# Full-height products, earlier maxima and a load behind a row of maxima in an attention stack

## The chip, the core and the metric

The kernel runs on one core of one Trainium2 chip. The metric is the device time of one execution in microseconds (us). TensorE's array has 128 rows; a product whose contraction has 64 terms uses 64 of them. TensorE's clock is granted at one of two levels, 1.2 or 2.4 GHz; the profile gives it as a share of the higher.

## The reference, cut to what matters

Four layers over 1024 tokens of width 256, each `x = x + attention(xn) + ffn(xn)` with `xn = layernorm(x)`. The change touches layer 0, and the order of work in layer 2. Layer 0's attention has 16 heads with low-rank queries and keys and a rotary part:

```python
ql, kvl = xn @ Wqd, xn @ Wkvd              # latents of 64 features each
q_nope, q_rope = ql @ Wqu, rope(ql @ Wqr)  # 16 and 64 features a head
k_nope, v = kvl @ Wku, kvl @ Wvu
k_rope = rope(xn @ Wkr)                    # one for all heads
# causal softmax of [q_nope q_rope].[k_nope k_rope], times v, times Wo
```

Beside it runs layer 0's second branch, again causal attention with 16 query heads against one key and value head that a router has selected for each token. Layer 2 has plain 16-head causal attention. Layer 1's feed-forward has a Hadamard transform, which the kernel folds into the weights `w_dn`.

## The kernel before, in words

All engines run their own instruction streams in order and meet at semaphores. Attention goes in groups of four heads: groups 0 to 7 in layer 0, even ones with the rotary part ("MLA"), odd ones of the shared key; groups 8 to 11 in layer 2. A group goes over eight key tiles, written (group, tile). For each tile TensorE writes scores to PSUM `psA` (MLA: lines 1678 and 1679), ScalarE writes their exponentials to `Pr` (lines 907 and 912), GpSimd masks the diagonal block (776), and TensorE multiplies the tile before by the values into `psO` (1716). Tiles 0 to 3 have four score units of up to 1024 queries, tiles 4 to 7 two of two heads each.

The softmax subtracts row maxima that come from a coarse pass of its own, done beside the tiles of the group before: 38 units a group, each a bf16 product (1661) into `psD` with a mask product (1663) on the diagonal, which VectorE reduces to `mx` (1199). `max_window` says beside which tiles the units go and `beside` spreads them by the queries left in each tile. At tile `MAX_END` = 5 the maxima are negated (1204), transposed (1669), copied to `mrow` (1217) and sent by a DMA in ScalarE's queue into the query operand, where they are a further row (926 and 929, `maxima_row`). The next group's first score waits for that DMA (`mrow_in`).

MLA operands come back from DRAM: SyncE's queue holds, for each even group i, the stores of two rotated tiles (`store_rotated`), a wait for the scores of (i, 3), `load_high(i + 2, 0)` (the high parts of the first 512 queries and keys, three DMAs: `Qr<-d_qr`, `Qr<-d_qn`, `Kr<-d_kn`), a wait for the group's last score, and then `load_high(i + 2, 1)` and all the rest. TensorE's `arrived(i + 2)` waits for the first three before the first maxima unit of group i + 2, which stands right behind the first score of (i + 1, 0).

Before group 0 the order is the list `PRE0`: the latents, the key rotation, two of four nope products, the rotated queries (four tiles, four `rope_unit`s each, f32 products in pairs, line 1595), and then the 38 maxima units of group 0 with other products among them: the values `v0` after unit 28, nope 1 after 31, nope 3 after 34. The four other tiles of rotated queries are made beside (2, 0), (2, 2), (4, 0) and (4, 2). Latents lie in one tile `lat`, queries in rows 0 to 63 and keys in rows 64 to 127. At the start of group 7 TensorE waits for GpSimd's butterflies (787) and makes four units of the Hadamard product (1759), which VectorE scales (1245).

Of the kernel before, what the change touches and what calls it, by code (L numbers as in the profile page):

```python
# [51 lines left out]
MAX_UNITS = list(max_units())  # L52
MAX_END = 5

# [21 lines left out]
def beside_products(i, kt):  # L76

    if (i, kt) in KV_AT:
        return [("kv", j) for j in KV_AT[i, kt]]
    if (i, kt) in ROPE_AT:  # L80
        return [("rope", ROPE_AT[i, kt], k) for k in range(4)]
    return []


def max_window(i, first):

    if i == 1:
        return [(0, kt) for kt in range(KEY_KT, MAX_END)]
    tail = [(i - 2, kt) for kt in range(MAX_END, NT) if i - 2 >= first and not is_mla(i)]
    return tail + [(i - 1, kt) for kt in range(MAX_END)]  # L90

# [23 lines left out]
def build(nc, ins, out):  # L115
    with ExitStack() as ctx:
# [119 lines left out]
        w_u, w_vu = part(D), part(D)  # L236
        w_o0, w_g0, w_qkv0 = part(DC, D), part(DC, H), part(DC, 3 * D)
        w_qkv0_at = 2 * DC * P + 2 * H * RD + 2 * D + DC * D + DC * H
        part = carve(WA)
# [138 lines left out]
        def d_attention(groups):  # L378

            names = [(f"max{groups[0]}", NMAX), (f"mrow{groups[0]}", 1)]  # L380
            for i in groups:
                nxt = i + 1 if i + 1 in groups else None
                if i == 2 * NG - 1:
                    names.append(("wdn", FC // 2))
                for kt in range(NT):
                    if nxt is not None and kt == MAX_END:
# [61 lines left out]
        dve_step, pool_step = sem("dve_step"), sem("pool_step")  # L448
        v_cleared, rotated = sem("v_cleared"), sem("rotated")
        ln_var, ln_std, xn_ready = sem("ln_var"), sem("ln_std"), sem("xn_ready")  # L450
# [30 lines left out]
        def _(sp):  # L481
# [13 lines left out]
            load(w_u[0:LAT, :], ins["Wqu"], w0_in)  # L495
            load(w_u[LAT:P, :], ins["Wku"], w0_in)
            load(w_vu[LAT:P, :], ins["Wvu"], w0_in)
# [91 lines left out]
            for i in GROUPS[0]:  # L589
# [4 lines left out]
                if is_mla(i) and i < 2 * NG - 2:  # L594

                    if i > 0:
                        store_rotated(i + 2)
                        store_rotated(i + 3)
                    sp.wait_ge(rope_stored, 16 * 2 * (i + 2))
                    sp.wait_ge(a_filled, scored(i, NT // 2 - 1))  # L600
                    load_high(i + 2, 0)
                    sp.wait_ge(a_filled, A[f"att{i}"])
                    load_high(i + 2, 1)
                    load_rest(i + 2, 0)
                    load_rest(i + 2, 1)
# [254 lines left out]
        def _(act):  # L860
# [31 lines left out]
            def attention(groups):  # L892
                for i in groups:
                    for kt in range(NT):
# [21 lines left out]
                        if (i, kt - 1) in ROPE_AT:  # L916
                            rope_cut(ROPE_AT[i, kt - 1])
                        if kt == MAX_END and i + 1 in groups:
                            maxima_row(i + 1)
# [199 lines left out]
        def _(dve):  # L1119
# [117 lines left out]

            def down_weights():

                dve.wait_ge(w1_in, 16 * N_W1)  # L1240
                for u in range(FC // 2):
                    src = take().rearrange("p (j d) -> p j d", j=2)
                    for k in range(2):
                        m = 2 * u + k
                        op = dve.scalar_tensor_tensor(w_dn[:, m, :], src[:, k, :], su[:, DC + m:DC + m + 1], ws_dp,
                                                      ALU.mult, ALU.mult)
                    op.then_inc(d_drained, 1)

# [11 lines left out]
            def attention(groups):  # L1260
# [6 lines left out]
                for i in groups:  # L1267
                    nxt = i + 1 if i + 1 in groups else None
                    if i == 2 * NG - 1:
                        down_weights()  # L1270
                    for kt in range(NT):
                        if nxt is not None and kt == MAX_END:
                            maxima_row(nxt)
                        for j in KV_AT.get((i, kt), ()):
                            if j == 0:
# [31 lines left out]
            def biased_times(dst, other, half, bias):  # L1307
# [3 lines left out]


            link(dve.memset(mx[:], LOWEST))
            stats()
            norm()
            dve.wait_ge(wq_high_ready, 1)
            dve.tensor_tensor(wq_low[0:LAT, :], WA[0:LAT, 2 * DC * P:2 * DC * P + 2 * T], wq_high[0:LAT, :],
                              ALU.subtract).then_inc(q_parts_ready, 1)
# [252 lines left out]
        def _(pe):  # L1571
# [173 lines left out]
            def attention(groups):  # L1745
# [7 lines left out]
                for i in groups:  # L1753
                    nxt = i + 1 if i + 1 in groups else None
                    if i == 2 * NG - 1:

                        pe.wait_ge(butterflies, 1)
                        for u in range(FC // 2):
                            pe.matmul(d_unit(), had[:], fT8[:, 2 * u:2 * u + 2, :].rearrange("p c d -> p (c d)"),
                                      start=True, stop=True).then_inc(d_filled, 1)  # L1760
                    if is_mla(i):
# [7 lines left out]
                    for kt in range(NT):  # L1769
# [12 lines left out]
                        def some_maxima(p):  # L1782
                            for unit in ahead[p * len(ahead) // points:(p + 1) * len(ahead) // points]:
# [3 lines left out]
                                if unit[0] == "kv":  # L1787
                                    selected_unit(unit[1])
                                    continue
                                if unit == MAX_UNITS[0]:  # L1790
                                    arrived(g)
# [3 lines left out]
                        for k, hs in enumerate(heads):  # L1795
                            one(hs)
                            if nxt is not None and kt == MAX_END:
                                if k == 1:
# [38 lines left out]
            def rope_unit(p, k):  # L1837
# [3 lines left out]
                product(d_unit(), [(wq_high[:, tile_cols(m)], lat_parts[:, c]),  # L1841
                                   (wq_low[0:LAT, tile_cols(m)], lat_parts[0:LAT, c])]).then_inc(d_filled, 1)

# [16 lines left out]
            pe.wait_ge(a_drained, A["xnT0"])  # L1860
            ql = lambda k, c: lat[0:LAT, c]
            kvl = lambda k, c: lat[LAT:P, c]
            for item in PRE0:
# [7 lines left out]
                elif item[0] == "nope":  # L1871
                    u = item[1]
                    pe.wait_ge(a_drained, A["lat"])
                    if u < 2:
                        features(lambda k: w_u[0:LAT, tile_cols(u)], ql, [0])
                    else:
                        features(lambda k: w_u[LAT:P, tile_cols(u - 2)], kvl, [0])
                elif item[0] == "v0":
                    value_units(kvl, lambda k: w_vu[LAT:P, :], [0])
                elif item[0] == "rope":  # L1880
# [238 lines left out]
```

## Time and profile before

| | us |
|---|---|
| median of 3 runs | 1012.65 (1007.17 to 1013.95) |
| the profiled execution, its own time | 1012.09 |
| its span | 1010.0 |
| mean granted clock of TensorE | 0.897 |

The span is from the first to the last instruction of the one profiled execution; 2.1 us lie around it. Everything read from the trace belongs to that execution. Landmarks on its time axis: PRE0 to 95, groups 0 to 7 from 95 to 478, groups 8 to 11 from 691 to 820.

### The profile page before, as it was taken

The page shows a single profiled execution, that of the slowest core. Times are in us where ns is not written, and L with a number is a line of the kernel's source. Part 1 is how long each engine was busy: PE and PEld are TensorE (multiplying, and loading weights), DVE is VectorE, ACT ScalarE, POOL GpSimd, SP SyncE. Part 2 cuts the span into 40 slices and gives each one's busy share as a digit, 9 for nine tenths or more (in the row PEclk, how much of TensorE's full clock was granted, in tenths as well). Part 3 has the DMA queues.
Part 4 walks back from the last instruction along what each step waited for, and adds up shares of the span by engine and source line. Part 5 has one row for each costly group of instructions (what it writes and reads, how often), then busy time and mean ns, then how long its engine had stood idle before and what let it go on. Part 6 is the DMA issues. An engine that isn't in the chain of part 4 may idle for free.

```text
span 1010.0 us, 11938 instructions
## 1 busy us (share of the span) xinstructions
PE 889.0 (88%) x4799; PEld 511.0 (51%) x4799; DVE 559.2 (55%) x988; ACT 387.0 (38%) x476; POOL 224.8 (22%) x207
## 2 busy tenths in 40 slices
PE   4998979999999899979589998977999889978997
PEld 2453534344334434424337877623333258778776
DVE  4583566774566367621443355496777426945452
ACT  2503424444443435445441431214556763500340
POOL 2381001323012301342210100400111236610010
PEclk9675999999698969989788998967999989979899
DMA  6675414532921390020400002477100051000001
GB/s 171 132 159 200 63 31 72 119 73 75 156 32 43 94 210 17 1 71 1 146 0 1 1 1 86 107 144 113 17 2 1 1 217 44 1 1 1 1 1 42
DMA packets 35647, 66.81 MB, mean 66 GB/s; under 512 B 5908, under 2 KB 14652, under 8 KB 35524
## 3 DMA queue, kind: packets, MB, share of 16 engines
q1 hardware_dynamic: 35016, 65.92, 28.3%
q8 instruction: 38, 0.62, 0.3%
q10 hardware_dynamic: 576, 0.13, 0.1%
q14 instruction: 17, 0.14, 0.0%
HBM read 45.93 MB, written 16.29 MB: 62 GB/s over the span
## 4 chain that ended last, share of the span: by engine, by line
PE 67%; DVE 19%; ACT 5%; DMA 4%; POOL 2%; issue 2%; SPq 1%; ACTq 0%; DVEq 0%; POOLq 0%
PE psD L1595 12%; PE psA L1595 11%; PE psO L1716 10%; DVE mx L1199 9%; PE psD L1661 9%; PE psO L1595 8%; PE psA L1679 7%; PE psA L1678 3%; DVE hid_low L1509 2%; PE psD L1663 2%; ACT Pr L907 1%; PE psA L1627 1%; DMA Kr<-d_kn 1%; ACT Pr L912 1%; PE psD L1727 1%
## 5 line engine op out<-in xcount | busy, mean ns | idle before, releaser
L1199 DVE TENSOR_REDUCE mx<-psD 128x1 f32<-128x512 f32 (+3 forms) x416 | 259.2, 658 | 127.8 <-PE psD L1663 91.1
L907 ACT ACTIVATE Pr<-psA 128x1024 f32<-128x1024 f32 (+3 forms) x192 | 161.8, 866 | 200.4 <-PE psA L1679 191.0
L776 POOL TENSOR_SCALAR_AFFINE_SELECT Pr<-Pr 128x512 f32<-128x512 f32 x96 | 60.9, 635 | 441.2 <-ACT Pr L907 355.1
L912 ACT ACTIVATE Pr<-psA 128x1024 f32<-128x1024 f32 (+3 forms) x96 | 63.5, 702 | 65.4 <-PE psA L1679 65.0
L1716 PE MATMUL psO<-Pr,Vh 128*32 128x512 f32 (+3 forms) x768 | 82.5, 510 | 3.7 <-POOL Pr L776 3.0
L1678 PE MATMUL psA<-Qr,Kr 128*128 128x512 f32 (+3 forms) x192 | 78.8, 424 | 2.8 <-DMA Qr<-mrow 2.8
L1663 PE MATMUL psD<-maskq,identb 128*128 128x128 bf16 x348 | 73.0, 234 | 0.0
L1679 PE MATMUL psA<-Qr,Kr 113*128 113x512 f32 (+3 forms) x192 | 67.1, 357 | 0.0
L1661 PE MATMUL psD<-Kr,Qr 80*128 80x512 bf16 (+3 forms) x166 | 60.2, 395 | 5.3 <-DVE mx L1199 3.0
L1661 PE MATMUL psD<-Kg,Qs 96*128 96x512 bf16 (+3 forms) x192 | 56.9, 337 | 8.6 <-DVE mx L1199 6.6
L1661 PE MATMUL psD<-Ks,Qs 96*128 96x512 bf16 (+3 forms) x166 | 53.5, 351 | 4.6 <-DVE mx L1199 3.9
L1679 PE MATMUL psA<-Qs,Kg 97*128 97x512 bf16 (+3 forms) x192 | 50.1, 357 | 7.2 <-DMA Qs<-mrowb 4.8
L1679 PE MATMUL psA<-Qs,Ks 97*128 97x512 bf16 (+3 forms) x192 | 45.8, 332 | 5.3 <-ACT Pr L907 3.3
L1678 PEld LDWEIGHTS psA<-Qr,Kr 128*128 128x128 f32 x192 | 37.9, 198 | 18.6 <-ACT Pr L912 6.1
L1661 PEld LDWEIGHTS psD<-Kg,Qs 96*128 96x128 bf16 x192 | 17.9, 97 | 58.0 <-DVE mx L1199 43.1
L1627 PE MATMUL psA<-identf,xn 128*128 128x128 f32 x96 | 21.6, 389 | 27.9 <-DVE xn L1164 27.4
L1661 PEld LDWEIGHTS psD<-Kr,Qr 80*128 80x128 bf16 x166 | 18.3, 111 | 52.0 <-DVE mx L1199 37.0
L1716 PE MATMUL psO<-Pr,Vg 128*32 128x512 f32 (+3 forms) x384 | 41.8, 516 | 1.2 <-POOL Pr L776 0.7
L1661 PEld LDWEIGHTS psD<-Ks,Qs 96*128 96x128 bf16 x166 | 16.5, 101 | 47.3 <-DVE mx L1199 42.4
L1679 PEld LDWEIGHTS psA<-Qr,Kr 113*128 113x128 f32 x192 | 37.9, 198 | 3.9 <-issue 1.7
L1663 PEld LDWEIGHTS psD<-maskq,identb 128*128 128x128 bf16 x348 | 36.7, 106 | 5.7 <-issue 3.2
L1595 PE MATMUL psA<-xnT,WA 128*128 128x512 f32 x56 | 31.3, 720 | 2.7 <-ACT xnT L872 2.2
(402 smaller groups left out, 1684.7 us busy)
## 6 DMA issues: line engine op xcount, KB each, us to landing
Qr<-d_qr SPq DMA_DIRECT2D x18, 512.0 KB, 12.3
d_qr<-WB SPq DMA_DIRECT2D x9, 512.0 KB, 2.6
Pr<-d_cb SPq DMA_DIRECT2D x8, 512.0 KB, 7.1
Qs<-d_gq SPq DMA_DIRECT2D x24, 128.0 KB, 4.7
Qs<-d_q SPq DMA_DIRECT2D x24, 128.0 KB
Ks<-d_k SPq DMA_DIRECT2D x24, 128.0 KB
Qr<-d_qn SPq DMA_DIRECT2D x18, 128.0 KB, 8.3
Kr<-d_kn SPq DMA_DIRECT2D x18, 128.0 KB, 9.2
```

The lines of the kernel that those rows point to most:

```text
L776: pool.affine_select(out=block_, in_=block_, pattern=[[0, GH], [1, P]], compare_op=ALU.is_ge, fill=0.0, base=0, channel_multiplier=-1).the ...
L907: act.activation(place[:, h, q0:T], src[:, q0:T], ACT.Exp, scale=score_scale(i)).then_inc(a_drained, 1)
L912: act.activation(place[:, h:h + 2, q0:T], src[:, :, q0 - HALF:HALF], ACT.Exp, scale=score_scale(i)).then_inc(a_drained, 1)
L1199: dve.tensor_reduce(mx[:, j, part, h0:h0 + nh], src, AX, ALU.max).then_inc(d_drained, 1)
L1509: dve.tensor_tensor(hid2_low[:, m - DC, :], slot(Qs, m - DC), hid2_high[:, m - DC, :], ALU.subtract).then_inc(hid2_split, 1)
L1595: op = pe.matmul(dst, lhsT, rhs, start=start and k == 0, stop=stop and k == len(terms) - 1)
L1627: op = pe.transpose(dst[:, tile_cols(j)], src[:, j, c * P:(c + 1) * P], identf[:])
L1661: op = pe.matmul(dst[:, k * w:(k + 1) * w], q, kk, start=True, stop=not diagonal)
L1663: op = pe.matmul(dst[:, (k + 1) * w - P:(k + 1) * w], identb[:], maskq[:], start=False, stop=True)
L1678: pe.matmul(out_, second[0], second[1](lo, (half + 1) * HALF), start=True, stop=False)
L1679: op = pe.matmul(out_, k, q(lo, (half + 1) * HALF), start=second is None, stop=not (diagonal and mask))
L1716: op = pe.matmul(psO[h * VW:(h + 1) * VW, lo:hi], values(i, kt, h), e, start=kt == 0, stop=kt == last_kt, tile_position=(0, h * VW), skip_ ...
```

## The change

- Full height. The lower-part weights of the queries' rotation are cut for all 128 rows, and the second product of each `rope_unit` takes 128 rows in place of 64 (the added rows multiply the low parts of weights and latents, a small term that was left out). The nope and value products take the whole of `lat`; the weights' other 64 rows are zeros, for which `Wku` moves to a place of its own (`w_ku`), VectorE issues three memsets at its start, and TensorE waits for them once (`zeros_ready`).
- Earlier maxima. `MAX_END` becomes `max_end(g)`: 5 for group 1, 4 for all others. Units before (g - 1, 4) come closer together, and the tail windows begin at tile 4. The row of maxima leaves one tile sooner.
- SyncE waits for the row of maxima of group i + 1 before `load_high(i + 2, 0)`.
- The four units of the Hadamard product go from the start of group 7 to beside (7, 1).

```diff
-MAX_END = 5
+def max_end(g):
+    return 5 if g == 1 else 4
...
+    if (i, kt) == (2 * NG - 1, 1):
+        return [("wdn", u) for u in range(FC // 2)]
     return []
...
     if i == 1:
-        return [(0, kt) for kt in range(KEY_KT, MAX_END)]
-    tail = [(i - 2, kt) for kt in range(MAX_END, NT) if i - 2 >= first and not is_mla(i)]
-    return tail + [(i - 1, kt) for kt in range(MAX_END)]
+        return [(0, kt) for kt in range(KEY_KT, max_end(1))]
+    tail = [(i - 2, kt) for kt in range(max_end(i - 1), NT) if i - 2 >= first and not is_mla(i)]
+    return tail + [(i - 1, kt) for kt in range(max_end(i))]
...
+        w_ku = WA[:, 6400:6400 + D]
...
-            load(w_u[LAT:P, :], ins["Wku"], w0_in)
+            load(w_ku[LAT:P, :], ins["Wku"], w0_in)
...
                     sp.wait_ge(a_filled, scored(i, NT // 2 - 1))
+                    sp.wait_ge(mrow_in, 16 * maxima(i + 1))
                     load_high(i + 2, 0)
...
-                        if kt == MAX_END and i + 1 in groups:
+                        if i + 1 in groups and kt == max_end(i + 1):
                             maxima_row(i + 1)
...
+            for w in (w_u[LAT:P, :], w_ku[0:LAT, :], w_vu[0:LAT, :]):
+                op = dve.memset(w, 0.0)
+            op.then_inc(zeros_ready, 1)
...
-            dve.tensor_tensor(wq_low[0:LAT, :], WA[0:LAT, 2 * DC * P:2 * DC * P + 2 * T], wq_high[0:LAT, :],
+            dve.tensor_tensor(wq_low[:], WA[:, 2 * DC * P:2 * DC * P + 2 * T], wq_high[:],
...
-                    if i == 2 * NG - 1:
-
-                        pe.wait_ge(butterflies, 1)
-                        for u in range(FC // 2):
-                            pe.matmul(d_unit(), had[:], fT8[:, 2 * u:2 * u + 2, :].rearrange("p c d -> p (c d)"),
-                                      start=True, stop=True).then_inc(d_filled, 1)
...
+                                if unit[0] == "wdn":
+                                    down_weights_unit(unit[1])
+                                    continue
...
-                                   (wq_low[0:LAT, tile_cols(m)], lat_parts[0:LAT, c])]).then_inc(d_filled, 1)
+                                   (wq_low[:, tile_cols(m)], lat_parts[:, c])]).then_inc(d_filled, 1)
...
-            ql = lambda k, c: lat[0:LAT, c]
-            kvl = lambda k, c: lat[LAT:P, c]
+            latents = lambda k, c: lat[:, c]
...
+                    pe.wait_ge(zeros_ready, 1)
...
-                    value_units(kvl, lambda k: w_vu[LAT:P, :], [0])
+                    value_units(latents, lambda k: w_vu, [0])
```

The new TensorE function waits for the butterflies and makes one unit; VectorE's `down_weights(u)` scales one, and both stand beside (7, 1), VectorE's ahead of the outputs of group 6:

```python
def down_weights_unit(u):
    if u == 0:
        pe.wait_ge(butterflies, 1)
    pe.matmul(d_unit(), had[:], fT8[:, 2 * u:2 * u + 2, :].rearrange("p c d -> p (c d)"),
              start=True, stop=True).then_inc(d_filled, 1)
```

## Rows read from the trace of the kernel before

**Rows 1.** The page: granted clock of TensorE in 40 slices, in tenths.

```profile
PEclk9675999999698969989788998967999989979899
```

**Rows 2.** The page: the chain that ended last, by engine.

```profile
PE 67%; DVE 19%; ACT 5%; DMA 4%; POOL 2%; issue 2%; SPq 1%; ACTq 0%; DVEq 0%; POOLq 0%
```

The columns of rows 3 and 9 are start:end and length; busy us (and instructions) of PE, PEld, DVE, ACT and POOL; granted clock; DMA share; GB/s.

**Rows 3.** Windows: rotation, values and nope, Hadamard product (two).

```profile
34.80:51.60 16.80, 16.80 (x24) 6.58 (x23) 8.57 (x13) 8.76 (x9) 9.02 (x4) 0.50 0.94 195
71.80:89.30 17.50, 17.50 (x34) 8.38 (x34) 9.32 (x15) 4.36 (x10) 5.74 (x4) 0.50 0.55 169
440.60:444.40 3.80, 3.78 (x5) 1.67 (x6) 0.88 (x2) 0.00 (x0) 0.55 (x1) 0.50 0.46 180
444.40:446.30 1.90, 1.90 (x4) 0.52 (x4) 1.75 (x4) 0.00 (x0) 0.00 (x0) 0.97 0.00 1
```

**Rows 4.** Timeline of TensorE, rotation before group 0 (start, length, us).

```profile
31.13 0.51 PE L1595 MATMUL psO<-lat_parts,wq_high 128*128 128x512 f32 x1
31.56 0.50 PE L1595 MATMUL psO<-lat_parts,wq_low 64*128 64x512 f32 x1
...
51.63 0.29 PE L1661 MATMUL psO<-Kr,Qr 80*128 80x128 bf16 x1
```

**Rows 5.** Timeline of SyncE's queue, and the landings of what it issued from 40.8 to 43.3.

```profile
40.87 2.44 SPq L483 DMA_DIRECT2D Kr<-d_kn  x1
...
Kr<-d_kn SPq DMA_DIRECT2D x1, 256.0 KB, 8.9
```

**Rows 6.** Timelines of TensorE and ScalarE's side, from the values to group 0.

```profile
71.78 7.19 PE L1595 MATMUL psA<-WA,OT 64*128 64x256 f32 x16
...
85.50 3.78 PE L1595 MATMUL psA<-OT,WA 64*128 64x512 f32 x4
...
93.02 0.59 ACTq L926 DMA_DIRECT2D Qr<-mrow  x1
...
95.41 0.77 PE L1678 MATMUL psA<-Qr,Kr 128*128 128x512 f32 x1 [2.81 <-DMA Qr<-mrow]
...
101.64 1.94 ACT L907 ACTIVATE Pr<-psA 128x1024 f32<-128x1024 f32 x2 [8.77 <-DMA d_gq<-Pr]
```

**Rows 7.** Timelines at group 0's end; landing of the `Kr<-d_kn` issued at 166.24.

```profile
161.08 0.54 ACTq L929 DMA_DIRECT2D Qs<-mrowb  x1
...
164.92 0.63 SPq L483 DMA_DIRECT2D Qr<-d_qr  x1
...
165.84 0.22 PE L1661 MATMUL psD<-Kr,Qr 80*128 80x128 bf16 x1
...
Kr<-d_kn SPq DMA_DIRECT2D x1, 128.0 KB, 6.8
```

**Rows 8.** Timeline of TensorE: a maxima unit in group 1, the start of group 3.

```profile
172.34 0.40 PE L1661 MATMUL psD<-Kr,Qr 80*128 80x512 bf16 x1
...
253.08 0.81 PE L1679 MATMUL psA<-Qs,Kg 97*128 97x512 bf16 x2 [2.38 <-DMA Qs<-mrowb]
254.81 0.29 PE L1661 MATMUL psD<-Kr,Qr 80*128 80x128 bf16 x1 [0.92 <-DMA Kr<-d_kn]
```

**Rows 9.** Windows: tiles 0 and 1 of groups 1 and 3; tile 2 of groups 2 and 4.

```profile
165.80:179.50 13.70, 12.41 (x86) 4.73 (x84) 11.32 (x19) 8.35 (x9) 1.83 (x3) 1.00 1.00 176
254.80:273.90 19.10, 18.39 (x85) 7.05 (x86) 11.59 (x19) 7.80 (x9) 0.70 (x2) 0.59 1.08 168
...
223.80:235.00 11.20, 9.98 (x51) 4.84 (x51) 8.77 (x14) 3.27 (x5) 1.93 (x3) 1.00 0.19 76
318.10:333.40 15.30, 14.28 (x51) 6.20 (x51) 8.78 (x14) 3.25 (x4) 1.50 (x2) 0.67 0.14 57
```

**Rows 10.** Timelines of GpSimd and TensorE, groups 6 to 7.

```profile
440.52 0.64 POOL L776 TENSOR_SCALAR_AFFINE_SELECT Pr<-Pr 128x512 f32<-128x512 f32 x1
440.62 5.87 PE L1759 MATMUL psD<-fT,had 128*128 128x512 f32 x8 [4.16 <-POOL fT L787]
...
448.71 0.43 PE L1716 MATMUL psO<-Pr,Vh 128*32 128x128 f32 x8
```

More of the change, by code:

```diff
@@ L382, in d_attention @@
                 nxt = i + 1 if i + 1 in groups else None
-                if i == 2 * NG - 1:
-                    names.append(("wdn", FC // 2))
                 for kt in range(NT):
-                    if nxt is not None and kt == MAX_END:
+                    if nxt is not None and kt == max_end(nxt):
                         names.append((f"mrow{nxt}", 1))
@@ L448, in build @@
         dve_step, pool_step = sem("dve_step"), sem("pool_step")
-        v_cleared, rotated = sem("v_cleared"), sem("rotated")
+        v_cleared, rotated, zeros_ready = sem("v_cleared"), sem("rotated"), sem("zeros_ready")
         ln_var, ln_std, xn_ready = sem("ln_var"), sem("ln_std"), sem("xn_ready")
@@ L1236, in outputs, with down_weights @@
                         stats((4 * b, 4 * b + 4))
-            def down_weights():
-                dve.wait_ge(w1_in, 16 * N_W1)
-                for u in range(FC // 2):
[L1242 to L1247, printed above, removed]
+            def down_weights(u):
+                if u == 0:
+                    dve.wait_ge(w1_in, 16 * N_W1)
+                src = take().rearrange("p (j d) -> p j d", j=2)
+                for k in range(2):
+                    m = 2 * u + k
+                    op = dve.scalar_tensor_tensor(w_dn[:, m, :], src[:, k, :], su[:, DC + m:DC + m + 1], ws_dp,
+                                                  ALU.mult, ALU.mult)
+                op.then_inc(d_drained, 1)
             def magnitudes():
@@ L1268, in attention @@
                     nxt = i + 1 if i + 1 in groups else None
-                    if i == 2 * NG - 1:
-                        down_weights()
                     for kt in range(NT):
-                        if nxt is not None and kt == MAX_END:
+                        if nxt is not None and kt == max_end(nxt):
                             maxima_row(nxt)
+                        if (i, kt) == (2 * NG - 1, 1):
+                            for u in range(FC // 2):
+                                down_weights(u)
                         for j in KV_AT.get((i, kt), ()):
@@ L1754, in attention @@
                     nxt = i + 1 if i + 1 in groups else None
-                    if i == 2 * NG - 1:
-                        pe.wait_ge(butterflies, 1)
-                        for u in range(FC // 2):
-                            pe.matmul(d_unit(), had[:], fT8[:, 2 * u:2 * u + 2, :].rearrange("p c d -> p (c d)"),
-                                      start=True, stop=True).then_inc(d_filled, 1)
                     if is_mla(i):
@@ L1796, in attention @@
                             one(hs)
-                            if nxt is not None and kt == MAX_END:
+                            if nxt is not None and kt == max_end(nxt):
                                 if k == 1:
@@ L1841, in rope_unit @@
                 product(d_unit(), [(wq_high[:, tile_cols(m)], lat_parts[:, c]),
-                                   (wq_low[0:LAT, tile_cols(m)], lat_parts[0:LAT, c])]).then_inc(d_filled, 1)
+                                   (wq_low[:, tile_cols(m)], lat_parts[:, c])]).then_inc(d_filled, 1)
+            def down_weights_unit(u):
+                if u == 0:
+                    pe.wait_ge(butterflies, 1)
+                pe.matmul(d_unit(), had[:], fT8[:, 2 * u:2 * u + 2, :].rearrange("p c d -> p (c d)"),
+                          start=True, stop=True).then_inc(d_filled, 1)
             def selected_unit(j):
@@ L1872, in _ @@
                     u = item[1]
+                    pe.wait_ge(zeros_ready, 1)
                     pe.wait_ge(a_drained, A["lat"])
[L1874 to L1877, printed above, removed]
+                    features(lambda k: (w_u, w_ku)[u // 2][:, tile_cols(u % 2)], latents, [0])
                 elif item[0] == "v0":
-                    value_units(kvl, lambda k: w_vu[LAT:P, :], [0])
+                    value_units(latents, lambda k: w_vu, [0])
                 elif item[0] == "rope":
```

## The prediction

> **What bounds the kernel now.** I read the chain of waits first: TensorE holds 67% of it, so its time counts wherever nothing else makes it wait [rows 2]. Then the slices of the granted clock [rows 1]: it is far under full in the second to fourth slice (25 to 100 us, PRE0) and again where groups 3 and 5 start. The windows show what TensorE did there. From 34.8 to 51.6 it was busy all the time at 0.50 of the clock, in the alternation of 128-row and 64-row products; from 71.8 to 89.3, again busy all the time at 0.50, in the values and nope products of 64 rows and six maxima units [rows 3]. The Hadamard product, 128 rows in f32 and little else, also began at 0.50 and was at 0.97 in the window that starts 3.8 us later [rows 3]. So here 64-row products left the clock low for 17 us, and dense 128-row ones got it back within about 4. A product's own time doesn't depend on its height: the 64-row one starts 0.43 us after the 128-row one and both last 0.5 us at full clock [rows 4].
>
> **Rotation before group 0.** 32 products run from 31.13 to 51.63 [rows 4]. At a pitch of 0.43 they would end at 44.8 if the clock stays up, 6.8 us sooner. But the first maxima unit needs `Kr<-d_kn`, issued at 40.87 and landed 8.9 us later, at 49.8 [rows 5], and this load hangs on ScalarE's copies of the nope products, which are made ahead of the slow stretch. So 5 us of the gain turn into a pause, and the pause may cost the clock, which then comes back as it did before. Taken: -1.8 us (51.63 to 49.8); bounds 0 (rotation stays slow) and -6.8 (the load moves up with it). VectorE's three memsets lie under the load of x: 0.
>
> **Values and nope.** 24 products: v0 takes 7.19 us, nope 3 3.78, nope 1 the same [rows 6]; 14.75 us at half clock. With 128 rows I let the first 4 us run slow (as the Hadamard product did) and the rest at full: 4 + (14.75 - 4) / 2 = 9.4, less 5.4; the maxima units between, three and three, go with them for another 0.2. That moves both things that group 0 waits for: the row of maxima, whose DMA is issued at 93.02 and which TensorE waits for until 95.41, and the store of split queries that ScalarE waits 8.77 us for [rows 6], because the stores behind nope 3 leave SyncE's queue in order. Group 0 then starts 5.6 us earlier, on top of the 1.8. Bounds 0 and -7.4 (all of it at full clock).
>
> **SyncE's new wait.** For groups 2 and 4 the row of maxima is sent about one tile sooner and `load_high` was held by its stores until then anyway: 0. For group 0 it is not. The row of group 1 is issued at 161.08 [rows 7]; the first row of maxima took 2.4 us from issue to the end of the wait (93.02 to 95.41) [rows 6], so the wait ends at 163.5; now the loads go out as soon as (0, 3) is scored. The third issue of such a group comes 1.3 us after the first (164.92, 166.24) [rows 7], which puts `Kr<-d_kn` at 164.8, and it lands 6.8 us later, as its sister at 166.24 did [rows 7]: at 171.6. TensorE wants it at 165.84 [rows 7] and stands, with all its queue behind `arrived(2)`: scores of (1, 0), the last values of group 0, and so ScalarE's exponentials. Price +5.8; bounds +3 (landing after 4 us) and +8. Queued on SyncE behind the wait are the second half and the rest; they go out a few tenths later, and the rest isn't needed until group 2: 0.
>
> A pause of this size has cost the clock before. At group 3 TensorE stood until 253.08 and again until 254.81 [rows 8], and its next two tiles took 19.1 us at 0.59 of the clock, where the same tiles of group 1 took 13.7 at 1.00 [rows 9]: 5.4 us. I add this, since 80-row maxima units follow in both: +5.4; bounds 0 and +5.4.
>
> **Earlier maxima.** Counting `beside` out, groups 1, 3, 5 and 8 get 48 units in place of 44, and 2, 4, 6 and 10 get 28 in place of 32. A unit's product lasts 0.40 us at full clock [rows 8]; overlap with its neighbours makes it cheaper, half clock dearer, and I take 0.4. What groups 2 and 4 save is not seen: the next group's first unit waits for `Kr<-d_kn` until 254.81, just after the wait for the row of maxima ends (253.08) [rows 8]. Removing the second wait there only uncovers the first; what remains is the first scores, 0.81 us, done in the pause, twice. Group 6 ends behind GpSimd's butterflies (below). Group 8 pays and group 10 gives back: 0. So 12 units at 0.4, 4.8 us, less 1.6: +3.2. Bounds -1.6 (units fit into gaps) and +5.6 (each costs a reduction of VectorE, 11.32 us for 19, 0.6 [rows 9]).
>
> **Rotation beside (4, 2).** Tile 2 of group 4 takes 15.3 us at 0.67 of the clock, tile 2 of group 2 with the same work 11.2 at 1.00 [rows 9]. With 128 rows I expect no fall: -4.1; bounds 0 and -4.1. The other three rotations ran at full clock: 0.
>
> **Hadamard product.** TensorE waits 4.16 us for the butterflies; GpSimd's mask of (6, 7) follows them at 440.52 for 0.64, and the values of (6, 7) run at 448.71 [rows 10]. In the new order the first two scores of group 7 are done in the wait, and these values start when the mask ends, 441.2: 7.5 us sooner. The four units return beside (7, 1), eight instructions at 0.43, or 3.4 us, and the clock will be low for about 4 us after the pause, in which some 1.7 us is lost that before fell on the product: -2.4. Bounds -7.5 (hidden under the exponentials) and 0. VectorE's scaling there goes ahead of group 6's outputs, wanted at tile 3 only: 0.
>
> **The sum.** -1.8 - 5.6 + 5.8 + 5.4 + 3.2 - 4.1 - 2.4 = +0.5. The profiled execution took 1012.09 (span 1010.0 and 2.1 around it), 0.6 under the median of 1012.65, so the forecast is 1012.6 on its scale and 1013 as a median. A measurement of this kernel can tell about 1% from no change, 10 us.
>
> **Rival 1, slower: rows don't move the clock.** The clock would follow busy time alone, rotation and values stay at half clock, and (4, 2) falls by chance. Then 1.8, 5.6 and 4.1 are missing: 1013 + 11.5 = 1024.5. Decisive is the window from 71.8: at 0.50 there, this case holds. Against it, those windows were busy 17.5 of 17.5 us at low clock, while the Hadamard product's clock rose [rows 3]; for it, tile 2 of group 2 held 1.00 with the 64-row products in it [rows 9].
>
> The Trainium skill ("TensorE: Matmul & The Clock Gate", What's actually happening) says that the gate is set by how busy TensorE has been recently, and says nothing of rows. By that rule this rival is right. The busy 17.5 us at half clock speak against it; no run here has yet shown the same product at both heights.
>
> **Rival 2: the pause at group 1 doesn't cost the clock.** It falls late, or comes back at once. For this: the falls follow no plain rule (of the tiles 2 of groups 2 and 4, alike in work, one fell) [rows 9]; against it stands group 3. 1013 - 5.4 = 1007.5.
>
> **Rival 3, faster: the change to the load does nothing.** If TensorE finds its operands at 165.84, because the row lands earlier or the loads, alone in the queue, in half the time, both 5.8 and 5.4 go: 1002.
>
> **How the numbers follow.** Forecast 0.50, rival 1 0.17, rival 2 0.17, rival 3 0.08, and 0.08 for falls of the clock elsewhere: their places move when work moves, and each such stretch is worth 3 to 5 us. Within the forecast the bounds of the terms mostly cancel; I give it 1006 to 1020. The range that leaves out 2 in 10 reaches over most of rivals 1 to 3: 1002 to 1023. Faster by over 1% (under 1002.5) takes half of rival 3 and a tail of rivals 2 and of low clock stretches that vanish: 0.20. Slower by over 1% (over 1022.8) takes most of rival 1 and a tail of the forecast: 0.19. The rest, 0.61, is within.
>
> **What the profile after would show.** The rotation ends near 45 us with a clock of 1.00, and TensorE waits for `Kr<-d_kn` until about 50; the clock rises in the values, and group 0's first score stands near 88 us. `Qr<-d_qr` for group 2 is issued after the first `Qs<-mrowb`, some 153 to 156 us, and TensorE has a wait of 5 to 6 us for `Kr<-d_kn` at the start of group 1, with a clock near 0.6 behind it. At groups 3 and 5 the wait for `mrowb` is gone and that for `Kr<-d_kn` is about 4 us. Tile 2 of group 4 takes 11 us. The values of (6, 7) come right after GpSimd's mask. Wrong it would be above all if the clock doesn't fall at group 1, if it stays low in PRE0, or if it is lost in stretches of layers 1 to 3 that the change doesn't touch.

## The result, and the profile after

The changed kernel takes 1016.23 us (median of 7 runs, 1011.90 to 1017.89), the kernel before, run beside it, 1007.17 us (median of 7 runs, 1005.26 to 1013.95; the three runs known at the forecast are among them). The ratio is 1.0073, with a 95% interval of 1.0048 to 1.0099: slower by 7 us, which is within 1% and clearly not nothing. Here and below, a difference in us is the ratio's, taken on the median of the kernel before, unless two medians are named; the medians themselves lie 9.1 us apart. The profiled execution took 1016.23 us, its span 1014.5.

The page of the kernel after: the granted clock in 40 slices, as in [rows 1], and the chain by engine, as in [rows 2].

```profile
PEclk9878996999799979979788998955999999989899
...
PE 62%; DVE 20%; DMA 6%; ACT 6%; POOL 3%; issue 2%; SPq 1%; ACTq 0%; DVEq 0%; POOLq 0%
```

The second to fourth slice have risen from 6, 7, 5 to 8, 7, 8, while TensorE's share of the chain fell from 67 to 62% and that of DMA rose from 4 to 6%. So work got faster and a transfer came onto the path. The waits of TensorE (us in total, times, longest) name it:

```profile
PE psD L1671 <- DVE mx L1205: 17.4, 61, 0.7
PE psD L1671 <- DMA Kr<-d_kn: 13.9, 3, 5.2
PE psO L1671 <- DMA Kr<-d_kn: 8.3, 1, 8.3
```

The first line is the wait for the reductions of maxima (`mx`); before, it was 13.5 us in 49 places. The four waits for `Kr<-d_kn` are the start of the maxima ahead of group 0 (8.3), and the starts of groups 1, 3 and 5.

TensorE's timeline of the kernel after, in PRE0 and at group 1, for [rows 4], [rows 6] and [rows 7]:

```profile
30.35 0.39 PE L1605 MATMUL psO<-lat_parts,wq_low 128*128 128x512 f32 x1
30.58 0.40 PE L1605 MATMUL psD<-lat_parts,wq_high 128*128 128x512 f32 x1
...
46.77 0.27 PE L1671 MATMUL psO<-Kr,Qr 80*128 80x128 bf16 x1 [8.34 <-DMA Kr<-d_kn]
...
67.70 6.22 PE L1605 MATMUL psA<-WA,OT 128*128 128x256 f32 x16
...
76.90 1.93 PE L1605 MATMUL psA<-OT,WA 128*128 128x512 f32 x4
...
161.28 0.29 PE L1671 MATMUL psD<-Kr,Qr 80*128 80x128 bf16 x1 [5.25 <-DMA Kr<-d_kn]
```

Rotation products now start 0.23 us apart at first and up to 0.34 later (0.43 before at full clock), the last at 38.05; but the first maxima unit starts only when `Kr<-d_kn` has landed, after a wait of 8.34. The nope 3 products take 1.93 us, not 3.78. At group 1 the pause for the late load is there. Windows of the kernel after, columns as in rows 3 and 9: rotation; the values and nope; group 1's start, and what follows.

```profile
34.80:51.60 16.80, 8.46 (x33) 4.76 (x33) 7.22 (x12) 8.13 (x8) 16.80 (x8) 0.72 1.05 202
62.00:72.00 10.00, 9.80 (x30) 5.15 (x30) 8.87 (x19) 0.75 (x3) 1.60 (x1) 0.53 1.02 161
72.00:82.00 10.00, 7.99 (x30) 4.03 (x28) 6.00 (x11) 7.00 (x12) 3.47 (x2) 0.96 0.54 218
...
155.00:162.00 7.00, 1.75 (x17) 0.85 (x11) 0.00 (x0) 1.37 (x2) 0.64 (x1) 0.73 1.04 192
162.00:176.00 14.00, 13.76 (x61) 5.16 (x60) 8.72 (x15) 5.76 (x6) 1.62 (x2) 0.53 1.08 172
```

The clock is at 0.96 from 72 to 82, where it was 0.50 before [rows 3]; and behind the pause at group 1 TensorE is busy for 14 us at 0.53, where tiles 0 and 1 of that group ran at 1.00 [rows 9].

To see where time goes and comes from, take the start of the first exponential of each group from ScalarE's timeline and cut the span there. The parts of a row add up to the span, to about 0.1 us. Group 8 is cut at the load of ScalarE's table just ahead of its first exponential (1.3 us ahead of it in every kernel), and "g6 to g8" holds groups 6 and 7 and all of layer 1. "Tile 2" is the time from the first exponential of tile 2 to that of tile 3 in groups 2 / 4, the place of a rotation whose clock fell in one kernel and held in another.

| kernel | start to g0 | g0 | g1 | g2+g3 | g4+g5 | g6 to g8 | g8 to the end | span | tile 2 |
|---|---|---|---|---|---|---|---|---|---|
| before | 101.6 | 64.5 | 37.7 | 94.3 | 98.5 | 294.6 | 318.8 | 1010.0 | 11.2 / 15.3 |
| after | 91.5 | 64.6 | 49.6 | 95.6 | 97.3 | 293.8 | 322.1 | 1014.5 | 12.1 / 12.1 |
| 1 after, no wait | 92.4 | 65.9 | 39.5 | 97.1 | 95.6 | 292.3 | 319.2 | 1002.0 | 12.1 / 10.6 |
| 2 height | 92.2 | 64.4 | 37.6 | 94.0 | 92.4 | 293.8 | 319.0 | 993.4 | 12.2 / 10.8 |
| 3 maxima | 98.7 | 64.7 | 39.5 | 101.3 | 99.6 | 295.2 | 317.8 | 1016.8 | 15.4 / 14.1 |
| 4 Hadamard | 97.1 | 64.8 | 37.7 | 94.3 | 96.5 | 293.7 | 318.7 | 1002.8 | 11.2 / 14.2 |
| 5 wait | 99.3 | 63.3 | 49.0 | 99.6 | 95.6 | 292.3 | 318.5 | 1017.6 | 15.3 / 11.2 |
| 6 rotation | 99.3 | 63.3 | 37.6 | 92.7 | 92.5 | 294.8 | 320.2 | 1000.4 | 10.7 / 10.8 |
| 7 values | 91.9 | 64.6 | 37.7 | 94.2 | 95.7 | 294.8 | 324.1 | 1003.0 | 11.1 / 14.1 |
| 8 height, two low | 94.0 | 64.5 | 37.6 | 94.4 | 92.0 | 294.3 | 319.6 | 996.4 | 12.2 / 10.7 |
| 9 fill | 88.4 | 65.7 | 37.6 | 94.0 | 92.4 | 294.4 | 319.5 | 992.0 | 12.2 / 10.7 |
| 10 fill, values | 92.4 | 63.5 | 37.7 | 91.5 | 90.9 | 293.6 | 319.7 | 989.3 | 10.8 / 10.7 |
| 11 maxima, g2 to g7 | 98.5 | 64.8 | 39.8 | 97.0 | 99.5 | 293.0 | 321.7 | 1014.3 | 11.1 / 14.1 |
| 12 late wait | 92.7 | 64.5 | 39.7 | 97.0 | 95.4 | 292.4 | 319.0 | 1000.7 | 12.1 / 10.6 |

Each row is one execution. Before to after: 10.1 us are won before group 0, 11.9 lost in group 1, and parts of both signs add 2.7. The largest of these is 3.3 from group 8 on, and it goes with a low-clock stretch of this execution: the first two tiles of group 8 take 18.6 us at a granted clock of 0.62 here, and 14.4 at 0.94 in kernel 12, which has the same maxima. Note also the 97.1 to 99.3 of kernels 3 to 6, whose values are as before: 2 to 4.5 us of the 101.6 are this execution's own clock.

### The profile page after: what moved, and what is told of

It reads as the page before. It is cut to its first block, busy times and chain, and to the rows that moved or that the text cites. A ratio compares the mean times of both kernels' runs of the same rounds, so it can differ in the third digit from the quotient of the medians.

```text
span 1014.5 us, 11941 instructions
## 1 busy us (share of the span) xinstructions
PE 875.5 (86%) x4799; PEld 507.7 (50%) x4799; DVE 557.6 (55%) x991; ACT 387.8 (38%) x476; POOL 224.8 (22%) x207
## 4 chain that ended last, share of the span: by engine, by line
PE 62%; DVE 20%; DMA 6%; ACT 6%; POOL 3%; issue 2%; SPq 1%; ACTq 0%; DVEq 0%; POOLq 0%
PE psA L1605 10%; PE psD L1605 10%; PE psO L1726 10%; DVE mx L1205 9%; PE psD L1671 9%; PE psA L1689 7%; PE psO L1605 7%; PE psA L1688 3%; DMA Kr<-d_kn 3%; PE psD L1673 2%; DVE hid_low L1519 2%; SPq L488 1%; ACT Pr L913 1%; PE psA L1637 1%; ACT Pr L918 1%
## 5 line engine op out<-in xcount | busy, mean ns | idle before, releaser
L918 ACT ACTIVATE Pr<-psA 128x1024 f32<-128x1024 f32 (+3 forms) x96 | 63.5, 702 | 57.1 <-PE psA L1689 56.2
L1673 PE MATMUL psD<-maskq,identb 128*128 128x128 bf16 x348 | 76.0, 242 | 0.0
L1671 PE MATMUL psD<-Kg,Qs 96*128 96x512 bf16 (+3 forms) x192 | 56.7, 335 | 10.8 <-DVE mx L1205 8.9
L1671 PE MATMUL psD<-Ks,Qs 96*128 96x512 bf16 (+3 forms) x166 | 57.1, 375 | 5.2 <-DVE mx L1205 4.1
L1689 PE MATMUL psA<-Qs,Kg 97*128 97x512 bf16 (+3 forms) x192 | 53.9, 381 | 4.2 <-POOL Pr L782 2.8
L886 ACT ACTIVATE ln<-ln 128x2 f32<-128x2 f32 (+1 forms) x10 | 2.0, 204 | 80.2 <-DVE ln L1160 80.2
```

Of the source, the lines that this page charges most:

```text
L918: act.activation(place[:, h:h + 2, q0:T], src[:, :, q0 - HALF:HALF], ACT.Exp, scale=score_scale(i)).then_inc(a_drained, 1)
L1671: op = pe.matmul(dst[:, k * w:(k + 1) * w], q, kk, start=True, stop=not diagonal)
L1673: op = pe.matmul(dst[:, (k + 1) * w - P:(k + 1) * w], identb[:], maskq[:], start=False, stop=True)
L1689: op = pe.matmul(out_, k, q(lo, (half + 1) * HALF), start=second is None, stop=not (diagonal and mask))
```

## The experiments

The whole is four things: the height, the sooner maxima, SyncE's wait, the place of the Hadamard product. Kernels 1 to 4 ran on one chip, 5 to 8 and 9 to 12 each on one, all in five rounds beside the kernel before (medians 1007.93, 1006.79, 1006.56).

**1. The kernel after without the wait.**

```
-                    sp.wait_ge(mrow_in, 16 * maxima(i + 1))
                     load_high(i + 2, 0)
```

> The changed kernel without SyncE's new wait. The theory (5.8 us of pause at the start of group 1 and 5.4 us of low clock behind it): TensorE finds Kr<-d_kn landed, group 1 takes some 38 to 39 us in place of 49.6, and the median falls by 11 us to 1005, just under the kernel before. If the pause costs no clock, only 5 to 6 us come back (1010). If the load was late anyway, nothing changes (1016).

Measured: 1002.51 us, ratio 0.9947 (0.9923 to 0.9971). The wait costs 1016.2 - 1002.5 = 13.7 us in the kernel after by the medians (12.7 by the two ratios), and without it the change is a gain. Group 1 takes 39.5 us in place of 49.6.

**2. The kernel before with all the 128-row products, nothing else.**

```
-                                   (wq_low[0:LAT, tile_cols(m)], lat_parts[0:LAT, c])])
+                                   (wq_low[:, tile_cols(m)], lat_parts[:, c])])
...
+                    features(lambda k: (w_u, w_ku)[u // 2][:, tile_cols(u % 2)], latents, [0])
...
-                    value_units(kvl, lambda k: w_vu[LAT:P, :], [0])
+                    value_units(latents, lambda k: w_vu, [0])
```

> The kernel before with full-height rotation, nope and value products alone. If the height of the products moves the clock: about 7 us less up to group 0 (2 at the rotation, since the load of the keys bounds it, and 5 in the values and nope products) and 3 to 4 where the clock no longer falls in group 4, so a ratio near 0.990. If the clock follows busy time alone: values and nope products stay at half clock and the ratio is 1.00 within 0.003, or a little over it, for nope 0 and nope 2 no longer run side by side.

Measured: 994.69 us, ratio 0.9882 (0.9847 to 0.9918), 11.9 us faster, with the clock in 72 to 82 at 0.94. This version beats both kernels.

**3. The kernel before with the maxima one key tile sooner, nothing else.**

```
-MAX_END = 5
+def max_end(g):
+    return 5 if g == 1 else 4
```

> The kernel before with the maxima one tile earlier alone. If each moved unit costs VectorE's 0.66 us where it comes and gives nothing where it goes (groups 1, 3, 5 and 8, four units each): 8 to 10 us more, less 1.6 for the first scores, so plus 7 to 8, ratio 1.007. If units fit into gaps: minus 1 to 2. My own forecast's term was plus 3.2.

Measured: 1016.34 us, ratio 1.0081 (1.0050 to 1.0112): 8.2 us slower, above the upper bound of its term, 5.6; the interval, 5.0 to 11.3 us, just reaches that bound.

**4. The kernel before with the Hadamard product beside (7, 1), nothing else.**

```
+    if (i, kt) == (2 * NG - 1, 1):
+        return [("wdn", u) for u in range(FC // 2)]
```

> The kernel before with the Hadamard product beside (7, 1) alone. Groups 6 and 7 took the same time in both profiles (80.2 and 80.1 us), so I expect no change, plus or minus 1 us: the values of (6, 7) run 7 us sooner, and a clock that stays low for some 14 us in place of 7 takes it back. The forecast's term was minus 2.4; if the clock recovers as early as before, minus 2 to 4.

Measured: 1008.16 us, ratio 1.0004 (0.9975 to 1.0033): nothing. Timeline of GpSimd and TensorE of the kernel after, for [rows 10]:

```profile
437.61 4.87 POOL L793 TENSOR_TENSOR fT<-WB 128x1024 f32<-128x1024 f32 x2
442.44 0.62 POOL L782 TENSOR_SCALAR_AFFINE_SELECT Pr<-Pr 128x512 f32<-128x512 f32 x1
...
443.12 1.03 PE L1689 MATMUL psA<-Qs,Kg 97*128 97x512 bf16 x2 [2.83 <-POOL Pr L782]
```

The mask of (6, 7) still stands behind the last butterflies in GpSimd's order, so the wait for the butterflies has become a wait for the mask (2.83 here, 3.85 in kernel 4). Behind it the clock is low, and attention is now what runs there: the window from 438.3 to 452 has 0.51. Group 7's first two tiles take 8.6 and 10.9 us in kernel 4, against 4.5 and 4.6 before, while group 6, up to the first exponential of group 7, takes 10 us less (40.5 in place of 50.5). What the Hadamard product paid before, they pay now.

**5. The kernel before with SyncE's wait alone** (the line of experiment 1, added).

> The kernel before with SyncE's new wait alone. Theory (the wait holds the load of split nope queries that group 1's first maxima product and first scores need, at group 0 alone, and the pause drops the clock behind it): TensorE pauses 4 to 6 us for Kr<-d_kn at the start of group 1, group 1 grows from 37.7 us to 48 to 50, and the total is 10 to 14 us above the kernel before, ratio 1.010 to 1.014; groups 3 and 5 unchanged. Rival (the 13.7 us which the wait cost in the kernel after exist only beside the full-height products or the earlier maxima, which move group 1's first maxima unit): less than 6 us, ratio under 1.006.

Measured: 1019.07 us, ratio 1.0130 (1.0099 to 1.0162), 13.1 us slower. TensorE's row at group 1:

```profile
168.42 0.29 PE L1662 MATMUL psD<-Kr,Qr 80*128 80x128 bf16 x1 [5.88 <-DMA Kr<-d_kn]
```

Group 1 grows from 37.7 to 49.0. The rival is out: the wait has its price without the other parts too. "Groups 3 and 5 unchanged" is half true: with the maxima at their old place the waits of SyncE at groups 2 and 4 let TensorE stand 5 us for `Kr<-d_kn` where it stood 2.4 and 0.9 [rows 8], and g2+g3 takes 99.6 us, 4.1 of that more in tile 2's clock and 1.2 here.

**6. The kernel before with the rotation alone at 128 rows** (the first pair of lines of experiment 2).

> The kernel before with the rotation products alone at 128 rows. Theory (a run of products of one height starts them 0.235 us apart, the alternation of 128 and 64 rows 0.43 us apart): the rotation ends near 38 to 42 us, TensorE waits for Kr<-d_kn until 47 to 50 us, group 0 starts 2 to 5 us sooner, the values before group 0 stay at half clock (v0 near 7 us), and the four rotations beside groups 2 and 4 give 1 to 3 us more: 3 to 7 us under the kernel before, ratio 0.993 to 0.997. Rival (the whole gain of the height is in the values and nope products, since TensorE waits for the load anyway): ratio within 0.002 of 1.

Measured: 1002.44 us, ratio 0.9961 (0.9940 to 0.9981), 3.9 us faster, but not at the place expected. Its profile can be held against that of kernel 5, whose rotation is as before, since the clock is 1.00 from 32 to 40 in both. TensorE in kernel 5:

```profile
30.26 0.50 PE L1596 MATMUL psO<-lat_parts,wq_low 64*128 64x512 f32 x1
...
43.07 0.49 PE L1596 MATMUL psD<-lat_parts,wq_low 64*128 64x512 f32 x1
48.47 0.26 PE L1662 MATMUL psO<-Kr,Qr 80*128 80x128 bf16 x1 [4.91 <-DMA Kr<-d_kn]
```

and in kernel 6:

```profile
39.58 0.40 PE L1595 MATMUL psD<-lat_parts,wq_low 128*128 128x512 f32 x1
48.37 0.26 PE L1661 MATMUL psO<-Kr,Qr 80*128 80x128 bf16 x1 [8.39 <-DMA Kr<-d_kn]
```

The rotation ends 3.5 us sooner and the next product starts 0.1 us sooner: the rest became wait, and group 0 starts at 99.3 in both. The gain lies beside groups 2 and 4: against kernel 4, whose clock fell in tile 2 of group 4 as that of the kernel before did, g2+g3 and g4+g5 take 5.6 us less, 3.4 of it in tile 2 of group 4 and 2.4 in the two tiles 0 (11.1 to 9.9 each).

**7. The kernel before with nope and value products alone at 128 rows** (the other lines of experiment 2).

> The kernel before with the nope and value products alone at 128 rows. Theory (the clock comes back in the stretch before group 0 once its products are 128 rows high): the values of key tiles 0 to 3 fall from 7.2 us to 6 or less, group 0 starts 4 to 6 us sooner, the rest is unchanged: 4 to 7 us under the kernel before, ratio 0.993 to 0.996; with the rotation alone it adds up to the 12 us that both gave. Rival (they work only together, since the pause for the load that follows the short rotation is what changes the clock's course): ratio within 0.003 of 1, and the two alone add up to less than half of 12 us.

Measured: 1001.63 us, ratio 0.9951 (0.9925 to 0.9977), 4.9 us faster. With experiment 6 that makes 8.8 of the 11.9 of both; with intervals of 2 to 3.6 us to each side of the three, the rest can be noise. The same window in kernel 6 (values of 64 rows) and in kernel 7 (128 rows), up to the end of the nope products:

```profile
72.00:80.00 8.00, 8.00 (x18) 4.47 (x17) 2.33 (x5) 2.42 (x8) 0.00 (x0) 0.50 0.78 285
```

```profile
72.00:80.00 8.00, 8.00 (x31) 4.41 (x29) 3.99 (x7) 5.00 (x11) 1.08 (x1) 0.93 0.79 287
```

TensorE is busy all the time in both, from 68 on; with 64 rows the clock stays at 0.50, with 128 rows it rises within the values and is 0.93 here. It isn't one lucky pair: from 73 to 80 the clock is 0.50 in all six kernels with 64-row values (before, 3, 4, 5, 6, 11) and 0.85 to 1.00 in the six with 128-row values and the old order before group 0 (after, 1, 2, 7, 8, 12). Nope 3 takes 3.78 us there and 1.93 here, for the same four products: the time of one follows the clock and not the rows, and at this place the clock goes with the rows. The first exponential of group 0 comes at 91.9 in place of 99.3.

**8. As 2, but the first two nope products kept at 64 rows.**

```
+                    if u == 0:
+                        features(lambda k: w_u[0:LAT, tile_cols(u)], ql, [0])
+                    elif u == 2:
+                        features(lambda k: w_ku[LAT:P, tile_cols(0)], kvl, [0])
```

> The kernel before with all products of the change at 128 rows, except the first nope products of the queries and of the keys, which stay at 64 rows in different halves of the rows (in the kernel before these eight took 1.99 us, in the kernel after 3.60). Theory (the load Kr<-d_kn hangs on these products through ScalarE's copies, and TensorE waits for it): the load is issued and lands up to 1.6 us sooner, and the total is 0 to 2 us under the kernel with every product at 128 rows, ratio 0.986 to 0.988 to the kernel before. Rival (the copies, not the products, set the load's time): the same as that kernel within 1 us, ratio 0.988 or more.

Measured: 996.44 us, ratio 0.9897 (0.9872 to 0.9922), no better than experiment 2. The eight products take 1.99 us and not 3.60, but from their start to the issue of `Kr<-d_kn` there are 11.7 us (28.52 to 40.20), in kernel 2 11.8 (27.14 to 38.97). The rival holds: something else on the way sets the load; which step it is wasn't tested.

**9. and 10. As 2, with products moved into the 8.4 us pause**: values and gq (9, shown), the values alone (10, `PRE0 += [("v0",)]`).

```
+        PRE0 += [("v0",), ("gq", 0)]
-        among = {2: ("gq", 0), 25: ("router",), 28: ("v0",), 31: ("nope", 1), 34: ("nope", 3)}
+        among = {25: ("router",), 31: ("nope", 1), 34: ("nope", 3)}
```

> The kernel before with all products of the change at 128 rows, and the values of key tiles 0 to 7 and the products of gq issued ahead of the first maxima product, in the 8.41 us for which TensorE waited there for Kr<-d_kn at the same height. Theory (that pause is idle time on the path, and these 24 products, 6.0, 5.0 us and the smaller rest, need nothing that comes later than its start): the wait shrinks to under 1 us, group 0 starts 5 to 9 us sooner than with the height alone (92.2), ratio to the kernel before 0.979 to 0.984. Rival 1 (VectorE's reductions bound the stretch of maxima that follows, 22 us of them from 52 to 82): half of it or less, 0 to 4 us, ratio 0.984 to 0.988. Rival 2 (the weights which gq needs aren't there yet, so that the wait moves to the loads): no gain or a loss, ratio 0.988 or more.

> As the kernel before this one, with the values alone issued in the pause, and gq where it was. Theory (pause time is worth what is put into it, up to its 8.4 us): group 0 starts 3 to 6 us sooner than with the height alone, ratio 0.982 to 0.985. Rival (the values kept TensorE's place while VectorE caught up with the reductions of the maxima, so that their removal only uncovers VectorE): 0 to 2 us, ratio 0.986 to 0.988.

Measured: 995.10 us, ratio 0.9881 (0.9857 to 0.9906), for 9, and 991.88 us, ratio 0.9855 (0.9831 to 0.9879), for 10. Kernel 9 missed its forecast: it is as fast as experiment 2 (0.9882). Its wait for the load is gone, but TensorE waits 3.89 us for ScalarE's copies of the values, and the first maxima unit starts at 52.19, in kernel 2 at 47.78. Kernel 10 has the lowest median, 14.6 us under the kernel before; with experiment 2 and with 9 the intervals overlap. It didn't gain where I expected either: the pause shrinks from 8.4 to 5.0 us, but group 0 starts at 92.4, as with the height alone (92.2). Two windows of kernel 10 behind the pause:

```profile
48.00:58.00 10.00, 8.87 (x40) 5.34 (x41) 3.21 (x6) 1.94 (x5) 10.00 (x5) 0.68 0.95 248
68.00:78.00 10.00, 8.32 (x19) 2.62 (x19) 7.41 (x18) 1.01 (x2) 0.00 (x0) 0.50 1.00 270
```

The 16 value products take 3.62 us in the pause and leave the later stretch, but there VectorE is busy 7.4 of 10 us, mostly with reductions, TensorE waits 1.7 us for one of them, the clock is now 0.50, and nope 3 ends at 80.2 (79.3 in kernel 2). Group 0 hangs on nope 3 through the stores behind it: from its end to the first exponential there are 11.4 to 12.9 us in the kernels before, after, 2, 9 and 10, and in 2, 9 and 10 ScalarE waits there for `d_gq<-Pr`, a store behind nope 3's. In kernel 9 it ends 2.3 us sooner, at 77.0, and group 0 starts 3.8 us sooner, 1.3 of which its first group gives back. Kernel 10's 3 us come as low-clock stretches that are missing in groups 2 to 5; whether they are its doing isn't settled. Nope 1 and 3 in the pause would be the next step, since group 0 hangs on them; it wasn't tried.

**11. The sooner maxima in groups 2 to 7 alone (layer 0).**

```
+    return 4 if 1 < g < 2 * NG else 5
```

> The kernel before with the maxima one key tile sooner in layers 0 and 1 alone (groups 2 to 7), layer 2 as it was. Theory (the 8.4 us that the sooner maxima cost in all layers lie in groups 1 to 5, where each unit that comes into a group with 44 costs what VectorE's reduction takes, while layer 2 only pays in group 8 what it gets back in groups 9 and 10): 7 to 9 us above the kernel before, ratio 1.007 to 1.009, group 8 back at 36.2 us. Rival (layer 2 carries a share): ratio under 1.006.

Measured: 1015.24 us, ratio 1.0092 (1.0061 to 1.0123). The whole cost is in groups 1 to 5, and layer 2 costs nothing that the runs can tell (1.0081 with it in experiment 3, 1.0092 without). Group 8 took 39.4 us here, not 36.2: in kernels 6, 7 and 11 its first two tiles ran slower with code as before, which is a clock stretch and no part of the change. Kernel 4 has the same clock in both tiles 2, so the cost can be read group by group: g1 +2.1, g2+g3 +2.7, g4+g5 +3.0, together 7.8. Tiles 2 and 3 of group 1 in kernel 4 and in kernel 11, at full clock:

```profile
177.00:187.40 10.40, 10.15 (x72) 3.42 (x70) 8.06 (x15) 5.84 (x9) 2.75 (x3) 1.00 0.68 127
```

```profile
179.60:192.30 12.70, 11.70 (x78) 3.82 (x75) 10.64 (x19) 5.85 (x9) 2.95 (x5) 1.00 0.49 93
```

Four more reductions, 2.6 us more of VectorE, 2.3 us more time, though TensorE has only 1.5 us more to do. A unit costs here what VectorE takes for it, 0.6 us.

**12. The kernel after, its wait left out at group 0 alone.**

```
+                    if i > 0:
+                        sp.wait_ge(mrow_in, 16 * maxima(i + 1))
```

> The kernel after, with SyncE's new wait left out for group 0 alone and kept for groups 2 and 4. Theory (the 13.7 us of the wait come from group 0 alone: at groups 2 and 4 the row of maxima is sent before the loads can go): within 2 us of the kernel after without any wait (1002.5), ratio to the kernel before 0.993 to 0.997, group 1 back from 49.6 to about 39.5 us. Rival (the waits at groups 2 and 4 add to the pauses of 4.5 us at groups 3 and 5): 3 to 6 us above it, ratio 0.998 or more.

Measured: 1003.22 us, ratio 0.9963 (0.9944 to 0.9983), beside 0.9947 without any wait. By the medians 13.0 of the 13.7 us come from group 0; at groups 2 and 4, with the sooner maxima, the wait costs nothing that these runs can tell (the two intervals overlap).

## Why the forecast was off by 7 us, step by step

The time is within 1% of the time before and inside the range, 3 us over the forecast's 1013. But part of that closeness is the reference: its median moved from 1012.65 of 3 runs to 1007.17 of 7, and against it +0.5 us was forecast and +7.4 came. By the parts measured alone (height -11.9, maxima +8.2, wait +12.7 to +13.7, Hadamard 0.4) one gets +9.4 to +10.4, at the upper end of the interval of the +7.4 (4.8 to 10.0). The forecast was too low for three of its four parts, the maxima most of all; that the time still fell near 1013 is in part luck with the reference.

- **Height, -1.8 - 5.6 - 4.1 = -11.5: right in sum (-11.9), and in part by luck.** The rotation before group 0 gave 0 and not -1.8: the -1.8 was gained on an execution whose clock happened to be low there (kernels 3 to 6 start group 0 at 97.1 to 99.3, not at 101.6, with the old values in place). The values gave 4.9 us of the time; group 0 starts at 91.9 with them and at 97.1 to 99.3 without. "The other three rotations ran at full clock: 0" was wrong, since **"a product's own time doesn't depend on its height: 0.43"** was read too far: it holds of the alternation of heights, where the weights are loaded only as the product ahead ends, and a pair takes 0.86 us; at one height it takes 0.47. That was worth 1.2 us in each tile 0.
- **-4.1 for (4, 2): 3.4 between kernels 4 and 6, but "I expect no fall" was wrong.** In the table the clock fell in 7 of the 12 tiles 2 with 64-row rotations (before, 3, 4, 5, 7, 11), in group 2 twice and in group 4 five times; such a tile takes 14.1 to 15.4 us at 0.66 to 0.76, and 11.1 to 11.2 without a fall. With 128 rows it fell in 7 of 16 (both of the kernel after; group 2 of 1, 2, 8, 9 and 12), but only to 0.86: 12.1 to 12.2 us, against 10.6 to 10.8. So 128 rows made the falls shorter and not clearly rarer; the kernel after has 12.1 us where the prediction looked for 11. Tile 2 of group 2 and of group 4 in kernel 2, alike in work:

```profile
213.00:225.20 12.20, 10.37 (x51) 4.89 (x49) 8.74 (x14) 3.24 (x4) 1.89 (x3) 0.86 0.18 71
307.00:317.80 10.80, 8.98 (x51) 4.53 (x50) 8.77 (x14) 3.28 (x5) 2.00 (x3) 1.00 0.21 82
```

- **The wait, +5.8 and +5.4: right mechanism, right place, 2 us short.** The pause was 5.25 us and the clock 0.53 behind it; group 1 of the kernel after lost 9.9 against kernel 12, that of kernel 5 11.3 against kernel 4. Of the rest, 3.1 us in the kernel after is the low-clock stretch in group 8 named above, and in kernel 5 what groups 2 and 3 lost; that the wait causes either isn't shown.
- **The sooner maxima, +3.2: the step that failed.** I took 0.4 us of TensorE for each of 12 units and set VectorE's 0.6 only as a bound of +5.6; and I took 1.6 off for scores done in the pause. Measured: +7.8 in groups 1 to 5. In the tiles that get the units VectorE is the engine that ends last (experiment 11), and the pauses at groups 3 and 5 didn't shrink: TensorE waits 4.1 to 4.5 us for `Kr<-d_kn` there, having waited 2.4 for the row and 0.7 to 0.9 for the load before. That the second wait uncovers the first was right; the 1.6 us for the first scores show in no total.
- **Hadamard, -2.4: 0.** The step "these values start when the mask ends, 441.2: 7.5 us sooner" moved the mask but not the low clock. I allowed 1.7 us for what falls on attention there; the window at 0.51 is 13.7 us long. The bound of 0 was in the text.
- **Rival 1 (rows don't move the clock) is refuted** for the values by experiments 6 and 7: same place, as busy, higher clock. What it says of tile 2 of group 4, a fall by chance, isn't refuted. The Trainium skill ("TensorE: Matmul & The Clock Gate", What's actually happening) speaks of busyness alone; by that rule the values would have gained nothing, and kernel 7 is 4.9 us faster. It isn't the whole story either way: kernel 10 has 0.50 in a stretch that holds 128-row nope products between 80-row maxima, and 128-row rotations didn't keep the clock up in 7 of 16 tiles.
- **Rivals 2 and 3** are out: the clock fell behind the pause, and the load came 5.25 us late.

## What to carry to other kernels

Run the parts of a composite change alone before you judge it: here a gain of 12 us lay under losses of 8 and 13. Price a moved unit by the engine that ends last in the tile that receives it, not by TensorE's share of it. And when a product is made faster ahead of a load, look at what the load itself hangs on, and move other work into the wait only if that work was not covering another engine.

## What the runs showed of the hardware that was not expected

- **Alternating heights.** At full clock, the rotation's 128-row products of 512 columns behind each other start 0.23 us apart; alternating with 64-row ones, 0.43. TensorE's weight loads (PEld) in kernel 5 say why: each begins only as the product ahead ends (from 29.83 for 0.50, an end that is modelled), while in kernel 6 it lies beside that product (from 30.09 for 0.39). This holds for the rotation, whose operands the kernel declares as float32r. The nope products, plain float32, start 0.43 us apart at full clock and one height (the eight in 3.60 us below).

```profile
30.26 0.18 PEld L1596 LDWEIGHTS psO<-lat_parts,wq_low 64*128 64x128 f32 x1 [0.24 <-issue]
30.69 0.19 PEld L1596 LDWEIGHTS psO<-lat_parts,wq_high 128*128 128x128 f32 x1 [0.25 <-issue]
```

```profile
30.10 0.19 PEld L1595 LDWEIGHTS psO<-lat_parts,wq_high 128*128 128x128 f32 x1
30.33 0.19 PEld L1595 LDWEIGHTS psO<-lat_parts,wq_low 128*128 128x128 f32 x1
```

The Trainium skill ("TensorE: Matmul & The Clock Gate", The mechanism) says in one sentence that a weight load overlaps running products only when its row group differs, and in another of the same section that a background weight buffer lets a load go ahead too. Kernel 6 is in line with the second and not with the first: it shows the load beside a product of the same rows; what isn't overlapped in the rotation is a load whose height differs from that of the product that runs.

- **The other way round,** 64-row products that take different halves of the rows ran side by side: eight in 1.99 us (kernel 8), in 3.60 us at 128 rows (kernel 2).

```profile
28.52 1.99 PE L1599 MATMUL psA<-OT,WA 64*128 64x512 f32 x8
```

```profile
27.14 3.60 PE L1599 MATMUL psA<-OT,WA 128*128 128x512 f32 x8
```

- **Low-clock stretches move between kernels with work that is the same**: with 64-row rotations, tile 2 of group 2 took 11.1 to 11.2 us in four kernels and 15.3 to 15.4 in two, that of group 4 11.2 in one and 14.1 to 15.3 in five. A difference of 3 to 4 us in one stretch of one execution says nothing about a change; the medians of five rounds do, or the same stretch in many kernels.
